# First attention: another order of the last maxima, of the turned score pairs and of the v and context evictions

## The reference, cut to what matters

```python
score = jnp.einsum('bhtsd,d->bhts', jnp.tanh(q[:, :, :, None, :] + k[:, :, None, :, :]), ws) + bs[0]
p_attn = jax.nn.softmax(score, axis=-1)
attn = jnp.einsum('bhts,bhsd->bhtd', p_attn, v)
attn = attn.transpose(0, 2, 1, 3).reshape(B, T, E)
return attn @ Wo.T + bo
```

## Time and profile before

| what | us |
|---|---|
| median of 3 runs | 1459.75 |
| lowest and highest of them | 1448.93, 1460.97 |
| the profiled execution's own time | 1448.74 |
| its span, first to last instruction | 1446.8 |
| mean granted clock of TensorE over the span | 0.943 |
| the first attention's tanh, first start to last end | 76.7 to 847.9 |

### The profile page before, as it was taken

The page is one execution under the profiler, slowest core; times in us unless marked ns, Lnnn a source line. Parts: engine busy times, 40 slices in busy tenths (PEclk is TensorE's granted clock), DMA queues, the critical chain, the costliest instruction groups (busy, mean ns, idle before and its releaser), DMA issues. The chain is left out here.

```text
span 1446.8 us, 39002 instructions
## 1 busy us (share of the span) xinstructions
PE 1153.0 (80%) x16164; PEld 874.5 (60%) x16164; DVE 1105.7 (76%) x2109; ACT 1003.6 (69%) x921; POOL 861.9 (60%) x978
## 2 busy tenths in 40 slices
PE   4766898788778887887788779847999999989496
PEld 3544665566556655665566458835667666767396
DVE  8797998899889998998899867753566677665443
ACT  1389999999999999999999967732234433433142
POOL 4098878887888788888888977540012222123354
PEclk9899999999999999999999999975899999988698
DMA  9999997000000000000000002000000100010352
GB/s 254 360 360 356 352 344 246 2 2 2 2 2 2 2 2 2 2 3 2 1 2 2 2 15 53 0 1 1 2 2 12 59 17 15 12 39 9 94 152 65
DMA packets 75449, 103.06 MB, mean 71 GB/s; under 512 B 6303, under 2 KB 73640, under 8 KB 75282
## 3 DMA queue, kind: packets, MB, share of 16 engines
q1 hardware_dynamic: 63784, 87.90, 18.5%
q10 hardware_dynamic: 6860, 6.12, 1.6%
q0 software_dynamic: 4640, 6.65, 1.4%
HBM read 18.32 MB, written 83.85 MB: 71 GB/s over the span
## 5 line engine op out<-in xcount | busy, mean ns | idle before, releaser
L917 ACT ACTIVATE work<-work 128x2864 f32<-128x2864 f32 (+1 forms) x272 | 688.8, 2578 | 32.2 <-DVE work L436 31.3
L436 POOL TENSOR_TENSOR work<-shared 128x1253 f32<-128x1253 f32 (+1 forms) x272 | 613.5, 2267 | 151.6 <-PE psum L1789 117.8
L1789 PE MATMUL psum<-work,ws_place 128*32 128x179 f32 x8640 | 397.6, 325 | 165.8 <-ACT work L917 165.6
L436 DVE TENSOR_TENSOR work<-psum,shared 128x1611 f32<-128x1611 f32 (+3 forms) x288 | 486.5, 1722 | 0.6
L1789 PEld LDWEIGHTS psum<-work,ws_place 128*32 128x32 f32 x8640 | 261.7, 112 | 274.4 <-ACT work L917 214.2
L1979 PE MATMUL psum<-shared 32*64 32x179 f32 (+1 forms) x1728 | 142.5, 367 | 8.1 <-DVE shared L1497 8.1
L756 POOL TENSOR_TENSOR tsum<-tstats 128x4 f32<-128x4 f32 (+1 forms) x16 | 3.7, 233 | 200.8 <-DVE tstats L1414 200.8
L1276 DVE SCALAR_TENSOR_TENSOR p_sb<-psum,bs_col,s_top 128x358 f32<-128x358 f32 x144 | 82.1, 570 | 43.9 <-PE psum L1802 30.7
L1979 PEld LDWEIGHTS psum<-shared 32*64 32x64 f32 (+1 forms) x1728 | 81.1, 159 | 56.5 <-issue 36.5
L1503 DVE TENSOR_SCALAR pt_region<-pt_region 128x1074 uint32<-128x1074 uint32 x48 | 34.6, 721 | 98.4 <-ACT pt_region L988 98.4
L906 ACT ACTIVATE pt_region<-psum,bs_neg 128x512 f32<-128x512 f32 x144 | 95.3, 663 | 1.6 <-PE psum L1802 1.5
(11 more groups left out here) (365 smaller groups left out, 1984.2 us busy)
## 6 DMA issues: line engine op xcount, KB each, us to landing
xs_dram<-pad_row SPq DMA_DIRECT2D x23, 3088.0 KB, 27.6
pt_region<-xs_dram ACTq DMA_DIRECT2D x19, 193.0 KB, 2.6
pt_region<-xs_dram SPq DMA_DIRECT2D x19, 193.0 KB, 2.4
xs_dram<-pad_row SPq DMA_DIRECT2D x1, 2895.0 KB, 27.0
work<-in_x SPq DMA_DIRECT2D x2, 768.0 KB, 10.1
work<-in_x ACTq DMA_DIRECT2D x2, 768.0 KB, 16.2
work<-in_L_ffn_W2T SPq DMA_DIRECT2D x1, 1536.0 KB
work<-in_L_ffn_W1T SPq DMA_DIRECT2D x1, 1536.0 KB
```

Of the source, the lines that this page charges most:

```text
L436: ins = eng.tensor_tensor(dst[:, a * KEEP:e * KEEP].rearrange("p (u s) -> p u s", s=KEEP), k[:, h * KP:h * KP + KEEP].unsqueeze(1).to_broa ...
L917: act.activation(a, a, ACT.Tanh).then_inc(tanh_done, 1)
L1789: ins = pe.matmul(bank_s[p % 2][32 * quad:32 * quad + 32, at:at + KEEP], ws_place[:, j, :], arg_slot(n)[:, u * KEEP:(u + 1) * KEEP], start ...
```

## The change

It moves calls to other groups; no instruction is added or left out.

- ScalarE: of the four exponentials that are left for the next round, the second (k = 6) is called at g = 1 in place of g = 2.
- VectorE: the two maxima left for the next round (k = 7 and 8) are called at g = 1 and 2 in place of g = 0 and 1; the two `ctx_keep` at g = 9 and 11 in place of 8 and 10, where they stand ahead of `pre_q` and `pre_k` of the same groups; `pre_v(b + 1)` at g = 16 becomes `pre_v(b)` at g = 0 of the next round, behind the sums of that group.
- TensorE: duo k is turned at g = 4 + 2k in place of 5 + 2k, so that seven duos (k = 0 to 6) in place of six are turned in their own round; k = 7 and 8 follow at g = 1 and g = 3 of the next, in place of k = 6, 7 and 8 at g = 0, 1 and 2.

```diff
--- before.py
+++ after.py
@@ -917,8 +917,8 @@
                         act.activation(a, a, ACT.Tanh).then_inc(tanh_done, 1)
                     if g % 2 and g >= 7 and real(b):
                         exps(b, (g - 7) // 2)
-                    if g in (0, 2, 3, 4) and real(b - 1):
-                        exps(b - 1, DUOS - 4 + (0, 2, 3, 4).index(g))
+                    if g in (0, 1, 3, 4) and real(b - 1):
+                        exps(b - 1, DUOS - 4 + (0, 1, 3, 4).index(g))
 
 
             act.preload_act_table(ACT.Gelu)
@@ -1321,10 +1321,10 @@
             def after_sums(b, g):
 
                 if real(b - 1):
-                    if g in (0, 1):
-                        smax(b - 1, DUOS - 2 + g)
-                    if g in (8, 10):
-                        ctx_keep(b - 1, (g - 8) // 2)
+                    if g in (1, 2):
+                        smax(b - 1, DUOS - 3 + g)
+                    if g in (9, 11):
+                        ctx_keep(b - 1, (g - 9) // 2)
                     if g == 12:
                         ctx_divide(b - 1)
                     if g == 14:
@@ -1341,8 +1341,8 @@
                         pre_q(b + 1)
                     if g == 11:
                         pre_k(b + 1)
-                    if g == 16:
-                        pre_v(b + 1)
+                if b and g == 0 and real(b):
+                    pre_v(b)
 
 
             pre_xT(0)
@@ -1821,8 +1821,8 @@
             def after_scores(b, g):
                 if real(b - 1):
                     c = b - 1
-                    if g in (0, 1, 2):
-                        turn_duo(c, DUOS - 3 + g)
+                    if g in (1, 3):
+                        turn_duo(c, DUOS - 2 + g // 2)
                     if g == 5:
                         pe.wait_ge(exp_done, DUOS * b)
                         pe.wait_ge(v_ready, b)
@@ -1852,8 +1852,8 @@
                             ins = product(bank_out[:, t * D:(t + 1) * D],
                                           [ctxT_wide[:, r, 128 * t:128 * t + 128] for r in range(2)], [wo0[:, r, :] for r in range(2)])
                         ins.then_inc(proj_psum, 1)
-                if real(b) and g % 2 and g >= 5:
-                    turn_duo(b, (g - 5) // 2)
+                if real(b) and g % 2 == 0 and g >= 4:
+                    turn_duo(b, (g - 4) // 2)
                 if real(b + 1):
                     if g == 3:
                         pre_turn(b + 1)
```

## The result

The changed kernel took 1438.65 us, the median of 4 runs (1436.34 to 1440.64), against 1459.53 us for the kernel before. The ratio of the means is 0.9872, with a 95% interval of 0.9822 to 0.9921: 1.3% less time, and the interval leaves out 1. The same kernel, run again later beside others on another occasion, had a median of 1429.25 us over 4 runs (1419.72 to 1441.77) against 1460.78, a ratio of 0.9768 (0.9705 to 0.9831), which leaves out the slowest of the four as a slow run. The first occasion agrees with the forecast of 1438.5 us and 0.985. On the second the medians lie 31.5 us apart, and 0.985 is above the interval: more was gained than forecast. The spread of this kernel over both occasions, 22 us, is as large as the gain.

The account below looks back on a forecast made before the run. ScalarE was taken to bound the first attention, with 1.36 us a round to give. The terms 20.4 + 1.5 - 0.75 = 21.2 us, subtracted from the median of 1459.75, gave 1438.5 us (0.985); range 1425 to 1450.

Parts of the forecast that it names:

- The wait and its size: Round start: turning duo 6 at g = 16 removes the group 2 tanh's wait; 1.36 us a round, 20.4 us in all.
- The cover of 0.2 us: TensorE's group 0 scores: their bank is free at about 608.3, against 608.5 for the tanh's end.
- The evictions: Moving `ctx_keep` and `pre_v`: no gain in a clean round; VectorE's wait moves to `pre_q`, about 1.2 us.
- the slack at group 13: VectorE's sums of group 13 are done 1.1 us before their tanh, before and after the change.
- The turns at even groups: TensorE in the round: a turn swaps with the context and the next with the q product; cost 0.
- Half clock: Attention rounds at 1.2 GHz: `pre_v` moved should cure the next round's late start; 0 to 2.9 us, 1.5 taken.
- the slack of the last exponential: Duo 8's exponential at g = 4 waits for its turn at g = 3, with 1.0 us of slack.
- The end: End of the first attention: `ffn_turn` holds back the last turn; 0.75 us lost, bounds 0 to 1.0.
- The total: Whole kernel: 21.2 us less, profiled execution 1427.5 us, median 1438.5 us, ratio 0.985.
- A: Rival: two buffers are too few in any order, VectorE's wait stays at L1276; gain 0, 1460.5 us; chance 0.06.
- B: Rival: the wait moves to group 13, losing 0.5 us of each 1.36; 1447.6 us; chance 0.12.
- C: Rival: half clock on groups 5 to 8 every round, 3.4 us lost where 1.36 are won; 1491 us; chance 0.03.

Follow-up runs that it names:

- experiment 1: Kernel before with only duo 6 turned at g = 16 of its own round instead of g = 0 of the next; 1447.74 us, ratio 0.992.
- experiment 7: Changed kernel with duos 0 to 5 turned at odd groups again, 1424.17 us; kernel before with only TensorE's turns moved, 1438.36 us.
- experiment 4: Kernel before with only `ctx_keep` moved to g = 9 and 11 and `pre_v` to g = 0; 1459.66 us in one run.
- experiment 5: Changed kernel with `ctx_keep` back at g = 8 and 10 and `pre_v` at g = 16; 1427.58 us, ratio 0.9801.
- experiment 8: Changed kernel with extra VectorE copies between the q product and the copies of q: two more, 1426.62 us; four more, 1442.45 us.
- experiment 2: The kernel of experiment 1 run again, nothing changed; 1437.76 us in one run.
- experiment 3: Kernel before with a third `p_sb` buffer and the wait before the subtraction loosened by one duo, no call moved; 1437.79 us in one run.
- experiment 6: Changed kernel run again, 1429.25 us; and changed kernel with the last duo turned at g = 2 in place of 3, 1439.68 us.

## Why the prediction was right, and where it was right by luck

**The wait and its size.** Right. Rounds of 46.80 us were forecast from the spacing of instructions, and 46.80 were measured; 20.4 us were the term, and the clean rounds give 15 x 1.36. The layout put the sums of group 2 2.0 us ahead of their tanh, and 1.72 were measured. The cover of 0.2 us at TensorE's scores of group 0 held: they start at 549.22, 0.45 us after the exponential that follows the tanh on ScalarE began (548.77), the same lag as in the next group (552.27 after 551.82). That the place of one turn caused it is shown by experiment 1 (its first clean rounds) and, for the whole, by turning alone in experiment 7.

**The evictions.** Right that they win nothing in a clean round (experiments 4 and 5: 48.16 stays 48.16, 46.80 stays 46.80). The wait moved to `pre_q` as forecast, but with 13.1 / 15 = 0.87 us and not 1.2, and the slack at group 13 is 1.37 us and not 1.1 (experiment 8). VectorE spends the rest of its free time at the maxima (L1273, 16.6 us in 21 waits), of which the prediction said nothing.

**The turns at even groups.** Costed at 0, with the argument that two swaps cancel. At full clock that holds, the rounds are 46.80 us with either (experiment 7). But with the wait removed, a kernel with odd turns and VectorE's old order loses up to 1 us in each of 8 to 12 rounds to half clock (experiments 1 to 3), and the changed kernel doesn't. The sum came out because the rest of the change comes with the turn of duo 6; I hadn't given that a price.

**Half clock.** I took 1.5 of 2.9 us. Measured: the changed kernel's rounds of 47.14 and 47.55 us together lose 1.1 us against 2.9 before, a gain of 1.8. The size came out for another reason than the one given. `pre_v` out of the way does cure the late start of the next round (experiment 4), but in the changed kernel there was nothing to cure: no stretch after round 0 fell at groups 5 to 8. That goes with the even turns (experiment 7), which I hadn't connected with it. A new loss stands at group 3, where I had put the slack of the last exponential at 1.0 us: a stretch takes it up, and that exponential is 0.3 and 0.7 us late in these two rounds.

**The end.** 0.75 us forecast, 4.63 - 3.88 = 0.75 measured, and experiment 6 removes it.

**The total.** The attention and its end give 22.07 - 0.75 = 21.3 us, forecast 21.2. But the profiled execution was to be at 1427.5 and was at 1436.3, because I held everything outside the first attention unchanged. (The start, 2.3 us longer, is also why the last tanh ended at 828.1 and not at 826.) In the second attention TensorE is busy 343 of 402 us, more than any other engine, and its clock differs from run to run. Its length times its mean granted clock is 351.8 us before and 351.8 after, and 348.1 to 352.3 in all eleven other profiles, while the length itself goes from 389.2 to 408.6 us and the clock from 0.905 to 0.852. (The constant of 341 us in my expectations was wrongly made: it counted a stretch that goes on beyond that part.) That the median came within 0.15 us is luck: in a kernel whose runs spread over 22 us it could have fallen elsewhere, as it did on the second occasion, 31.5 us under the kernel before where my terms allowed 23.3 at most. The sentence that nothing else varies was true of the first attention only. Of 18 timed executions of the kernel before, one took 1448.9 us and the others 1457 to 1463. That fits a second attention of differing length, but only the execution of 1448.7 us was profiled, so whether the change also makes the second attention faster on average is open.

**The rivals.** A is refuted by every run in which duo 6 is turned at g = 16 with two buffers. B and C didn't happen in the changed kernel. B was near: with scores at half clock, one of the conditions that it named, the wait did move to group 13 in experiments 1 to 3, and their slowed rounds lose three quarters of the 1.36 us again. For C's mechanism, series of stretches at groups 5 and 6, experiments 1 to 3 are the case; it costs 0.99 us a round where I had 3.4, and stays on the winning side. What I drew from the Trainium skill's rule that idleness brings the throttle (TensorE: Matmul & The Clock Gate, Part 1), that an order with less waiting has fewer stretches, was right for the changed kernel (8.5 and 8.7 us of idle time a round in its two profiles against 9.7 before, 5 and 3 stretches against 8). It failed in experiment 1: TensorE is idle less there too (8.6 us; 8.9 to 9.0 in the rounds without a stretch, 10.4 before), and it has more stretches, 13 against 8.

## What to carry to other kernels

Where one wait repeats in each round, look at the place of the instruction that ends it in its own engine's order: here one transposition, queued behind the scores of a group that it didn't need, held VectorE and through it ScalarE, and moving that one call gave back 1.36 us a round without a buffer. Then look at the times of the single rounds and not only at the sum: here rounds fell in step with TensorE's low-clock stretches, each one or each fourth. And split a total at marks that both traces have before trusting a difference: here a stage that nobody touched moved by up to 19 us.

## What the runs showed of the hardware that was not expected

Half-clock stretches of TensorE, 3.41 us long by the trace, returned 47.78 to 47.79 us apart for 12 rounds in two runs of one kernel, and for 8 in another, where the rounds took 47.6 to 48.1 us. In one profile each of three more kernels, the changed one among them, they returned 187.73 us apart, with every fourth round. The spacing stayed the same where the rounds differed; what sets it was not found.

The second attention, the same instructions in all kernels, ran at mean granted clocks of 0.852 to 0.905. What decides it wasn't found: among kernels that reach it within 4 us of each other (931 to 935 us) it took 389 to 409 us.
